# Two mixtures of experts: the tables of the passes read into registers eight numbers at a time

## The reference: what is computed

```python
# layer 2 (gated; each expert takes at most `capacity` tokens for each k)
gate = silu(einsum('ecd,efd->ecf', disp, wi_gate))
up = einsum('ecd,efd->ecf', disp, wi_up)
expert_out = einsum('ecf,edf->ecd', gate * up, wo)
out = out + where(valid[:, None], ew[:, None] * tok_out, 0.0)
# layer 3 (ungated; every token that chose the expert)
h = gelu(x @ w1_i, approximate=False)
acc = acc + cw[..., None] * (h @ w2_i)
```

## Time and profile before

| | us |
|---|---|
| median of 3 runs | 1251.55 |
| lowest and highest of the runs | 1249.97, 1255.73 |
| the profiled execution | 1258.5 |
| its span, from the first to the last instruction | 1257.2 |
| loop of layer 2, from its first product to the last scatter's issue | 831.4 to 954.8 |
| loop of layer 3, the same | 1125.6 to 1236.0 |
| busy: PE 915.5, PEld 533.2, DVE 899.7, ACT 578.6, POOL 547.4 | |

### The profile page before, as it was taken

One profiled execution on the slowest core, in us unless ns is written; L12 is line 12 of the kernel. 1 busy time (PEld: TensorE's weight loads), 2 busy tenths in 40 slices (PEclk: granted clock), 3 DMA queues, 4 the chain that ended last, 5 costly groups with the idle time before them and its releaser, 6 DMA issues.

```text
span 1257.2 us, 18690 instructions
## 1 busy us (share of the span) xinstructions
PE 915.5 (73%) x5207; PEld 533.2 (42%) x5207; DVE 899.7 (72%) x1700; ACT 578.6 (46%) x1232; POOL 547.4 (44%) x553
## 2 busy tenths in 40 slices
PE   6977787888666866678889888679893850558782
PEld 3522234333344552222223322469893530547682
DVE  6679999999999377877887871754455589972223
ACT  3478663665132443146776668334342740223232
POOL 2068995999401323201112211245534585235643
PEclk9879898999877988679998999679996775669896
DMA  8000000000000301311110100511102000011113
GB/s 294 1 1 1 1 0 1 1 1 1 1 0 1 134 1 53 98 27 27 27 28 27 27 2 2 201 62 35 39 27 78 1 0 1 9 42 36 41 33 113
DMA packets 28018, 46.32 MB, mean 37 GB/s; under 512 B 8721, under 2 KB 16409, under 8 KB 26897
## 3 DMA queue, kind: packets, MB, share of 16 engines
q1 hardware_dynamic: 22672, 34.67, 8.6%
q0 software_dynamic: 4096, 8.35, 2.2%
q10 hardware_dynamic: 1152, 2.10, 0.4%
HBM read 34.46 MB, written 12.58 MB: 37 GB/s over the span
## 4 chain that ended last, share of the span: by engine, by line
PE 39%; DVE 30%; issue 11%; ACT 8%; POOL 5%; DMA 3%; another core or an unknown queue 2%; SPq 1%; DVEq 0%; ACTq 0%; POOLq 0%
PE ps L2798 9%; PE ps L2807 5%; PE ps L1821 5%; PE ps L1803 4%; DVE sb_hs L756 3%; POOL sb_gs L926 3%; DVE sb_l_mxp L1935 2%; PE ps L1748 2%; DVE sb_xn L168 2%; DVE sb_stats L145 2%; ACT sb_l_rc L2228 1%; PE ps L1756 1%; ACT sb_l_pT L1878 1%; DVE ps L718 1%
## 5 line engine op out<-in xcount | busy, mean ns | idle before, releaser
L1935 DVE TENSOR_REDUCE sb_l_mxp<-ps 128x2 f32<-128x1024 f32 (+3 forms) x152 | 171.5, 1163 | 41.5 <-PE ps L1748 40.2
L926 POOL TENSOR_TENSOR sb_gs<-sb_hs,sb_xp 128x512 f32<-128x512 f32 x128 | 163.2, 1294 | 23.2 <-DVE sb_hs L756 21.1
L1878 ACT ACTIVATE sb_l_pT<-ps 128x512 f32<-128x512 f32 (+3 forms) x256 | 111.4, 521 | 76.8 <-PE ps L1803 75.7
L2798 PE MATMUL ps<-sb_hT,sb_f_shared 128*128 x936 | 127.5, 288 | 13.6 <-ACT sb_f_shared L2815 6.8
L605 PE MATMUL ps<-sb_gs,sb_ident 128*128 128x512 f32 x256 | 133.8, 605 | 1.0 <-POOL sb_gs L926 0.7
L2798 PEld LDWEIGHTS ps<-sb_hT,sb_f_shared 128*128 128x128 f32 x936 | 116.6, 200 | 22.2 <-issue 22.2
L2868 DVE SCALAR_TENSOR_TENSOR sb_f_rows<-ps,sb_f_mask,sb_f_rows 128x128 f32 x78 | 27.4, 351 | 116.6 <-PE ps L2807 57.0
L1803 PE MATMUL ps<-sb_l_qk 51*128 51x512 bf16 (+3 forms) x384 | 89.3, 335 | 19.0 <-ACT sb_l_pT L1878 7.8
L2896 POOL DMA_INDIRECT moe_y<-sb_f_rows,sb_f_rowi x64 | 63.8, 997 | 82.4 <-DVE sb_f_rows L2868 69.7
L2807 PE MATMUL ps<-sb_sw_f_out,sb_f_hid 128*128 x624 | 86.3, 283 | 14.0 <-ACT sb_f_hid L2837 9.3
L2837 ACT ACTIVATE sb_f_hid<-ps 128x512 f32<-128x512 f32 x78 | 46.5, 596 | 103.3 <-PE ps L2798 75.9
(11 more groups left out here) (394 smaller groups left out, 2046.8 us busy)
## 6 DMA issues: line engine op xcount, KB each, us to landing
sb_sw_f_in<-w_f_in SPq DMA_DIRECT2D x2, 2048.0 KB, 10.1
sb_sw_f_out<-w_f_out SPq DMA_DIRECT2D x2, 2048.0 KB, 13.1
sb_l_qk<-spill SPq DMA_DIRECT2D x112, 32.0 KB
spill<-sb_l_parts SPq DMA_DIRECT2D x12, 256.0 KB, 2.9
moe_y<-c_f_zero SPq DMA_DIRECT2D x1, 2048.0 KB, 9.8
sb_sw_f_up<-w_f_up SPq DMA_DIRECT2D x1, 2048.0 KB, 12.1
moe_h<-sb_f_rows SPq DMA_DIRECT2D x8, 256.0 KB, 5.2
sb_f_rows<-moe_y SPq DMA_DIRECT2D x8, 256.0 KB, 6.1
```

The lines of the kernel that those rows point to most:

```text
L926: gp.tensor_tensor(gs[:, q % SL, :], hs[:, q % SL, :], cs[:, k % 2, hf * CH:(hf + 1) * CH], ALU.mult).then_inc(times_c, 1)
L1878: ac.activation(pT[e % 3][:, h, 0:width], ps[:, bank[n_bank], 0:width], ACT.Exp, scale=L2_SCALE).then_inc(exped, 1)
L1935: dv.tensor_reduce(dst, src, AX_X, ALU.max).then_inc(max_out, 1)
L2798: m = pe.matmul(ps[:, 2 * (i % 2) + n, fs], own[:, i % 2, n, fs], xr[:, bass.ds(r, 1), :], start=True, stop=True)
```

## The change

`at_index` no longer reads one number. The first time that an engine asks for a number of a table in a group of eight, the whole group (the last one has seven) is read into registers by one TENSOR_LOAD, and the registers are kept in `held`; later requests of the group find theirs there. The range checks (the register operation and the assertion after each read) are left out.

```diff
+        AT_ONCE = 8
 
         def at_index(e, table, i, n):
-            return e.value_load(table[0:1, i:i + 1], min_val=0, max_val=n - 1)
+            key = (e.engine, table.name, i // AT_ONCE)
+            if key not in held:
+                i0 = i // AT_ONCE * AT_ONCE
+                _, held[key] = nc.values_load_multi_w_load_instructions(
+                    table[0:1, i0:min(i0 + AT_ONCE, NPASS)], engines=(e.engine,), min_val=0, max_val=n - 1,
+                    skip_runtime_bounds_check_because="the tables are counts ...")
+            return held[key][i % AT_ONCE]
...
         td_at, at_block, at_mask, at_zero = [], [], [], []
+        held = {}
```

More of the change, by code:

```diff
@@ L2774, in experts @@
         TURN_BANK, Y_BANK = (6, 5), (7, 4)
+        AT_ONCE = 8
         def at_index(e, table, i, n):
-            return e.value_load(table[0:1, i:i + 1], min_val=0, max_val=n - 1)
+            key = (e.engine, table.name, i // AT_ONCE)
[3 more added lines that the diff above has]
+                    table[0:1, i0:min(i0 + AT_ONCE, NPASS)], engines=(e.engine,), min_val=0, max_val=n - 1,
+                    skip_runtime_bounds_check_because="the tables are counts of at most NE - 1 edges and blocks masked or clipped to their range")
+            return held[key][i % AT_ONCE]
         def keep_busy():
```

## The result

| | before | changed |
|---|---|---|
| median of 20 runs each | 1255.62 us | 1249.34 us |
| lowest and highest | 1249.97 to 1261.84 | 1241.17 to 1255.08 |
| ratio of the two | | 0.9962, 95% interval 0.9945 to 0.9979 |
| profiled execution, its span | 1258.5, 1257.2 | 1250.68, 1249.2 |

By the ratio the change makes the kernel faster by 0.38%, which is 4.8 us, with 2.6 to 6.9 us as the interval. The two medians lie further apart, by 6.3 us (0.9950); both values lie in the interval, and I go by the ratio. The interval doesn't include zero, but the gain is less than the 0.5% from which the prediction called a version faster. The forecast was 8.4 us less and 1243.2 us, the range 1237 to 1253. The time lies in the range, but 6.1 us above the point. Of these 6.1, the kernel before accounts for 4: its median over 20 runs is 1255.62 and not 1251.55, as it was over three.

The account below looks back on a forecast made before the run. PE's instruction queue was taken to bound much of layer 3, with no engine busy throughout. 5.6 + 2.8 + 1.0 - 1.0 = 8.4 us less, from 1251.55 to 1243.2 us; range 1237 to 1253.

Parts of the forecast that it names:

- passes 3 to 12: Start of layer 3: seven of nine intervals lose 0.4 us each without single reads and checks, 2.8 us less.
- passes 12 to 24: Middle of layer 3, where POOL's cycle may set the time: 1.0 us less, with 0 and 4.8 as ends.
- passes 24 to 38: Last third of layer 3: the matrix unit becomes the bound, 25.4 us instead of 31.0, a gain of 5.6 us.
- layer 2: Layer 2's loop: matrix unit full or holds rule, reads are off the chain; gain zero.
- cost of the reads of eight: PE's later group reads of `x_at`: six may outlast the queue's lead, charged at 1.0 us.
- PE's queue as the bound of layer 3: Layer 3's last 15 passes: 2.21 us an interval against 1.79 of matmuls; reads with checks hold 1.2 to 1.3.
- middle of two far bounds, 1.35 us: Assumed length of a read of eight on PE, between one read, 0.30 us, and eight, 2.4.
- lead of 1.3 us: How long a read of `x_at` in PE's queue may last before it shows, in both layers: 1.3 us.
- rival built on nearly eight reads: PE's queue: a read of eight costs 2.05 us, gain only 2.1 us, time 1249.4; chance 0.22.
- Next in line is POOL ... They stay hidden.: Last third of layer 3: POOL's scatter of 1.0 + 0.3 us a pass, below 1.79, and DVE and ACT don't show.
- POOL takes the gain: Layer 3: faster PE lengthens POOL's issue rows and holds; one 3 us hold added, 1.6 less, 1250; chance 0.13.
- the same difference gives 1243.2 us: Whole kernel: profiled 1258.5 becomes 1250.1; the runs' median lies 7 us lower, 1251.55, so 1243.2 timed.

Follow-up runs that it names:

- g1: The kernel before, without an edit, run and profiled once more in the third session, which had no holds; 1231.66 us (one run).
- g2: The changed kernel, without an edit, timed again in the third session, which had no holds; 1219.78 us, ratio 0.9913 to the kernel before.
- f2: Changed kernel without POOL's later work (gathers from the 19th block on, all scatters but the last), second session; 1212.60 us, ratio 0.9880 to before.
- i2: Changed kernel without gathers from the 19th block on and all scatters but the last, fifth session; 1213.96 us, ratio 0.9859 to before.
- e3: Changed kernel, but PE reads single numbers with checks as before; DVE and ACT read groups of eight without; 1252.87 us, ratio 1.0000 to before.
- g3: Changed kernel with AT_ONCE = 1: one number at a time, each kept, without the range checks; 1221.69 us, ratio 0.9926 to before.
- e1: Changed kernel, but each table's last group is read as the eight numbers 31 to 38; 1252.58 us, ratio 0.9993 to before.
- f3: Changed kernel with a POOL memset of 128 x 512 after each of the later gathers; 1228.00 us, ratio 0.9981 to before.
- i3: Changed kernel with 22 gathers ahead of the first scatter instead of 18, fifth session, without holds; 1214.89 us, ratio 0.9872 to before.
- h1: Changed kernel with 22 gathers ahead of the first scatter instead of 18, fourth session, with holds; 1245.19 us, ratio 0.9893 to before.
- i4: The changed kernel, without an edit, once more in the fifth session, without holds; 1218.72 us, ratio 0.9906 to before.

## Why the prediction was half right

Layer 3's terms, in us, against the profiles with holds and without:

| | forecast | with holds | without (g1, g2) |
|---|---|---|---|
| passes 0 to 3 | 0 | -2.4 | -0.4 |
| passes 3 to 12 | -2.8 | -2.7 | -3.9 |
| passes 12 to 24 | -1.0 | -1.2 | -0.9 |
| passes 24 to 38 | -5.6 | -2.6 | -4.6 |
| layer 2 | 0 | -1.5 | -0.4 |
| cost of the reads of eight | +1.0 | not seen | 0.2 at most (f2, i2) |
| timed, by the ratio | -8.4 | -4.8 | -10.7, -11.6 |

The first column of profiles is not made of gains alone. e3, whose PE reads one number at a time as before, has -2.5, -0.3, -2.1 and +0.9 in the same four stretches, which is scatter between executions or between holds.

**PE's queue as the bound of layer 3: right.** e3 and g3 show it from both sides. With PE's reads as before nothing is gained; without the checks alone all of it comes.

**The reads of eight: right in effect, the size was off.** The middle of two far bounds, 1.35 us, stood for 0.59. So the 1.0 us that the sum charged for them wasn't paid: f2 and i2, with POOL's work gone and the reads in place, took 25.6 and 25.4 us for the last third, the 25.4 of the forecast without a charge. The lead of 1.3 us was not measured itself; it lies between the 1.07 us that didn't show in i2 and the 2.0 us that came through in e1. The Trainium skill, page "Runtime: NRT & Kernel Launch", section "Instruction fetch mechanics", has 200 ns for each register even in bulk, an estimate of 1.6 us for eight; here eight took 0.59 us and sixteen 1.1 when they started at a multiple of eight, and eight from number 31 took 2.0. For the groups of this kernel the measurement decides, and the page's figure is too dear. The rival built on nearly eight reads (1249.4) met the time by luck.

**The step that failed: "Next in line is POOL ... They stay hidden."** I took POOL's price for the last third from its scatters alone, 1.3 us a pass, below 1.79. But once PE is faster, the stretch with gathers reaches into the last third (in g2 the intervals up to pass 27 still stand at 2.6, POOL's pair of issues), and in the sessions with holds the last third gets a hold where there was none. Of the 5.6 us forecast there, 2.6 came in the first comparison's profile and 4.6 without holds: 3.0 and 1.0 were lost. For the 1.0 POOL is shown as the cause, by f2, f3 and i3. For the 3.0 it is not: the two long intervals stand beside POOL's issues, but no run took these away in a session with holds, and moving four gathers ahead (h1) left the stretch at 28.6. The rival "POOL takes the gain" had named a new hold of 3 us in the last third and was given 0.13. That rival's chance was too low for how well it describes the result. i3 confirms the mechanism without holds: with POOL's order mended, the stretch meets the forecast to 0.1 us.

**A gain that wasn't forecast:** the first three intervals of layer 3, 2.4 us in the first profiles and 0.4 without holds. e3 has it too (7.6 us against 10.1) without a change to PE's reads, so it is not the change's.

**From the profile to the time.** The single profile gave 8.3 us in layer 3, but the timed runs 4.8 by the ratio. That 8.3 meets the 8.4 of the forecast is luck: what the last third lacks is made up by the first three intervals, the reads that cost nothing and scatter. A second step that failed is "the same difference gives 1243.2 us", one profile of the kernel before as the base of the sum: with PE's reads as before, e3's layer 3 loop took 113.7 us, not 117.7, at the same timed ratio of 1.000. Six profiles with grouped reads on PE in sessions with holds give 109.1 to 110.3. Against e3 the loop's gain is 3.4 to 4.6 us, near what the clock shows, though e3 too is one execution. A stretch ruled by holds varies between executions, and I had read its length from one.

**What stays open:** what a hold is. Shown is that holds are in the time without a profile (24 us between sessions), that they need neither the checks nor single reads, that the clock was at half behind one of the longest, and that a chip has them in one session and not in another. The ends of PE's products are modelled in the profile, so it can't tell a late release from a product that really ended late. That they go with POOL's rows of issues was read from traces only; no run without those issues fell into a session with holds. Why the first comparison's ratio differs from the later ones is put down to the holds because the profiles show them at that place; it is not shown. i4 at 0.9906 against 0.9962, with intervals of 0.9869 to 0.9942 and 0.9945 to 0.9979, just parts them; but the first comparison's medians give 0.9950, which lies outside i4's interval by less than 0.001, and h1 stands at 0.9893 in a session with holds.

## What to carry to other kernels

Where an instruction queue, not its engine, sets the pace, what stands between the operations counts: the checks behind a register read cost about as much as the read here (0.3 us each), and once the queue was below the engine's own time, more savings there brought nothing that could be told. Before forecasting a gain, add up the next engine's work over the whole loop, not over the stretch where it looks idle: POOL's 83 us stood in a loop that shrank to 91 where there were no holds. And where a profile shows late starts without a releaser, profile the same kernel in another session before any length of those stretches is used; here a tenth of the two loops' time, 28 of 249 us, went with them.

## What was not expected of the hardware

- A read of table numbers into registers by its group: one number 0.30 us, eight from a multiple of eight 0.59, sixteen 1.1, but seven (32 to 38) 1.07 and eight from number 31 2.0.
- Releases of PE that come late by up to 4.6 us in one session and not at all in another, on the same chip and with the same kernel, worth 24 us of 1255. (In the first profile a second product is done at 1163.57 by the trace, and DVE's addition that waits for it starts at 1168.14.)
- Behind 3.6 us in which PE stood, its granted clock was at 0.50 for at least 2.5 us, and a first product took 2.07 us instead of 1.15.
- Four more gathers issued first, with the same instructions in all, gave PE 4.5 us in a stretch of 27.
